# Cross-attention, two layers: new orders around o, and the low parts made on VectorE

## The chip, the cores and the metric

The kernel runs on 1 core of one Trainium2 chip. The metric is the device time of one execution in microseconds (us). The kernel before takes 1041.25 us, the median of 3 runs (1039.71 to 1041.26).

## The reference

x is (32, 224, 512), the context is (32, 750, 256), all in float32. Two layers follow each other; each computes, for every batch,

```
q = emb @ Wq + bq;  k = latent @ Wk + bk;  v = latent @ Wv + bv
w = softmax(q @ k.T / sqrt(512), axis=1)      # over the 224 rows of q, not over the context
x = w @ v + emb
out = (x - mean(x)) * rsqrt(var(x) + 1e-6) * gamma + beta
```

The second layer takes the first one's output as emb and the same context. Each has its own weights.

## The kernel before, in words

**Folding.** Wq and Wk are folded once into A, so that "q" is x times A with 256 columns, and scores are that q times the raw context. The values are folded too: first o = w @ context (256 columns), then o @ Wv, called pv. The bias of v is added with the row sum r of the probabilities.

**High and low parts.** Most products are split to keep float32 accuracy. A tensor t has a high part t_hi in the format fp32r, and t_lo = t - t_hi. A product is hi*hi + hi*lo + lo*hi. The high part is a conversion and the low part a subtraction that must see the high one finished. For o, only the first three of six chunks of 125 context rows are split: p_hi, p_lo (125x672, one buffer each) and raw_hi, raw_lo (125x384 for each half l of the columns, two slots by batch). The other three chunks are multiplied as they are.

**Units and turns.** A unit is one batch in one layer. A turn handles one unit of layer 0, called a, and one of layer 1, called b, which belongs to an earlier batch (in code a(+0) and b(+0), with a(-1), b(-1) for the turn before). There are 32 units of each layer. Some turns are written out, the middle ones are a loop of two turns. The first units and the last two have shapes of their own (opening, front_o_product, last_o_product).

**Order.** Each engine has a hand-written list, `turn(i, j)`, and runs it strictly in order. Semaphores tie the lists together. The steps that matter:

- TensorE (`turn` of the tensor block): score_product of a in three pairs of chunks, o_product of the earlier b (second half), two transposes of b's x, the pv and q products, then o_product(a, 0), spread_d(b), score_product(b, 0), (b, 1), o_product(a, 1), score_product(b, 2), q_product(a(+1), 0), pv_product(a, 0), spread_d, pv_product(a, 1), q_product(a(+1), 1), o_product(b, 0).
- VectorE takes the maxima of the scores (score_max, L1443), makes xT_lo (L1395), cT_lo, qT_lo (q_lo, L1426), oT_lo, the reciprocals (invert_sum, L1463), p_hi (probs_hi, L1479), raw_hi (L1491), the dots with a weight row (L1416), adds pv (add_pv, L1542), takes the moments (half_moments, L1559), and turns blocks of x and the context (turn_x, turn_ctx).
- ScalarE makes the high parts of transposed data, the exponentials (exps, L1023), scales the probabilities by the reciprocal (normalise, L1045), and standardises (L1080).
- GpSimd makes p_lo (L1864) and raw_lo (L1872), sums the probabilities (L1881 to L1896), takes the power -1/2 (L1941), and applies gamma and beta (L1958, L1967). SyncE issues the DMAs.

The waits of an o product are what the change touches most. o_product writes oq_bank[l], which has held the q of the next unit, so it first waits until VectorE has read that (q_lo):

```
if u.at(1).real:
    pe.wait_ge(qT_lo_done, u.n(1, 2, l - 1))
...
if u.layer == 0 or u.first:
    pe.wait_ge(raw_lo_done, u.batch(LC, l + 1))
if l == 0:
    pe.wait_ge(p_hi_done, u.n(add=-1))
```

Then it waits for the normalised second half of the probabilities ahead of L745, and for p_lo ahead of L749. q_product of b waits at L691 for xT_lo of b, its first half ahead of the first two products of the low part and its second half ahead of the other two. A GpSimd or VectorE step that needs the result of a step before it on the same engine waits for its semaphore as well.

Of the kernel before, what the change touches and what calls it, by code (L numbers as in the profile page):

```python
# [5 lines left out]
ALU = mybir.AluOpType  # L6
ACT = mybir.ActivationFunctionType
F32 = mybir.dt.float32
# [80 lines left out]
def build_xattn(nc, x, ctx, weights, out):  # L89
    B, T, E = x.shape  # L90
    _, M, L = ctx.shape
    P = 128
# [13 lines left out]
    with ExitStack() as stack:  # L106
# [821 lines left out]
        def _(act):  # L928
# [54 lines left out]
            def xT_hi_part(u, g):  # L983
                if not u.real:
                    return
                if u.layer:
                    act.wait_ge(xT_ready, u.batch(2, g + 1))
                    src = t_bank[0][:, 0:2 * T].rearrange("p (e t) -> p e t", e=2)
                else:
                    act.wait_ge(x_turned, u.batch(2, g + 1))  # L990
                    src = first_x(g) if u.first else turned_x(u, g)
                if u.past(-2) and g == 0:

                    act.wait_ge(q_ready, u.n(-2, 2))
                act.activation(xT_hi[:, u.par, 2 * g:2 * g + 2, :], src, ACT.Identity).then_inc(xT_hi_done, 1)  # L995
# [115 lines left out]
            def turn(i, j):  # L1111
                a, b = units(i, j)
                ctxT_hi(a(-1), 2)
                d_out(a(-1))
                standardise(a(-2), 0)
                standardise(a(-2), 1)
                ctxT_hi(a(-1), 3)
                o_hi(b(-2), 1)
                xT_hi_part(b(-1), 0)
                seed(b(-2), 1)  # L1120
                exps(a(-1), 0)
                xT_hi_part(b(-1), 1)
                xT_hi_part(a(+0), 0)
                exps(a(-1), 1)
                q_hi(b(-1), 0)
                normalise(a(-1), 0)
                normalise(a(-1), 1)
                q_hi(b(-1), 1)
                xT_hi_part(a(+0), 1)
                o_hi(a(-1), 0)  # L1130
                d_out(b(-1))
                seed(a(-1), 0)
                seed(a(-1), 1)
                exps(b(-1), 0)
                o_hi(a(-1), 1)
                standardise(b(-2), 0)
                standardise(b(-2), 1)
                ctxT_hi(a(+0), 0)
                q_hi(a(+0), 0)
                normalise(b(-1), 0)  # L1140
                exps(b(-1), 1)
                normalise(b(-1), 1)
                q_hi(a(+0), 1)
                ctxT_hi(a(+0), 1)
                seed(b(-1), 0)
                o_hi(b(-1), 0)
# [76 lines left out]
            seed(b29, 1)  # L1223
            exps(a31, 0)
            xT_hi_part(v, 1)
            exps(a31, 1)
            q_hi(v, 0)
            normalise(a31, 0)
            normalise(a31, 1)
            q_hi(v, 1)  # L1230
            o_hi(a31, 0)
# [45 lines left out]
        def _(dve):  # L1277
# [194 lines left out]
            def probs_hi(u):  # L1472

                if not u.real:
                    return
                dve.wait_ge(probs_done, u.n(m=2, add=-1))

                dve.wait_ge(o_ready, u.n(-1, 2))
                dve.tensor_copy(p_hi[0:MP, :, :], probs[0:MP, u.par4, 0:HALF, :]).then_inc(p_hi_done, 1)  # L1479

            def raw_hi_part(u, l):
# [8 lines left out]
                    dve.wait_ge(raw_loaded[u.slot][l], u.turns(16))  # L1490
                dve.tensor_copy(raw_hi[0:MP, u.slot, :, cols], raw[0:MP, u.slot, 0:HALF, cols]).then_inc(raw_hi_done, 1)  # L1491

            def take_r(u):

                if not u.real or not seeded(u):
                    return
                dve.wait_ge(oT_hi_done, u.n(m=2, add=R_HALF - 1))
                dve.wait_ge(y_done, u.n(-2, 2))
                dve.tensor_copy(r_col[0:TP, u.par, :], r_psum).then_inc(r_taken, 1)
# [114 lines left out]
            def turn(i, j):  # L1614
# [12 lines left out]
                score_max(b(-1), 4)  # L1627
                score_max(b(-1), 5)
                ctxT_lo(a(+0), 0)
                probs_hi(b(-1))  # L1630
                add_pv(a(-1), 0)
                q_lo(a(+0), 0)
                turn_ctx(a(+0), 1)
                invert_sum(b(-1), 1)
                half_moments(a(-1), 0)
                add_pv(a(-1), 1)
                half_moments(a(-1), 1)
# [20 lines left out]
                take_r(b(-1))  # L1658
                invert_sum(a(+0), 0)
                raw_hi_part(a(+0), 0)  # L1660
                score_max(a(+0), 5)
                xT_lo_part(b(+0), 1)
                dot(b(+0), 0)
                add_pv(b(-1), 0)
                q_lo(b(+0), 0)
                invert_sum(a(+0), 1)
                raw_hi_part(a(+0), 1)
                dot(b(+0), 1)
                probs_hi(a(+0))
                half_moments(b(-1), 0)  # L1670
                xT_lo_part(a(+1), 0)
                turn_x(a(+1), 1)
# [40 lines left out]
            turn_x(a1, 0)  # L1713
            o_lo(a0, 0)
            raw_hi_part(a0, 0)
            raw_hi_part(a0, 1)
            sum_beta(2)
            o_lo(a0, 1)
            sum_beta(3)
# [30 lines left out]
            score_max(a1, 5)  # L1750
            invert_sum(a1, 0)
            raw_hi_part(a1, 0)
            raw_hi_part(a1, 1)
            turn_x(a2, 0)
            fold_c(1, 1)
            xT_lo_part(b0, 1)
# [4 lines left out]
            dot(b0, 1)  # L1761
            q_lo(b0, 1)
            probs_hi(a1)
            xT_lo_part(a2, 0)
            turn_x(a2, 1)
            o_lo(a1, 0)
# [67 lines left out]
        def _(pool):  # L1834
# [10 lines left out]
            def first_sum_probs():  # L1845
                halves = [(probs[0:MP, 0, 0, :], 1), (psum3[0:MP, 0, :], 2), (psum3[0:MP, 0, :], 3), (psum3[0:MP, 0, :], 4),
                          (psum3[0:MP, 0, :], 5)]
                for k, (of, c) in enumerate(halves):
# [6 lines left out]
                        pool.tensor_tensor(psum_all[0:MP, :], of, probs[0:MP, 0, c, :], ALU.add).then_inc(psum_done, 1)  # L1855
                    else:
                        pool.tensor_tensor(psum3[0:MP, 0, :], of, probs[0:MP, 0, c, :], ALU.add).then_inc(first_psum_done, 1)

            def probs_lo(u):

                if not u.real or u.first and u.layer == 0:
                    return
                pool.wait_ge(p_hi_done, u.n(add=-1))
                pool.tensor_tensor(p_lo[0:MP, :, :], probs[0:MP, u.par4, 0:HALF, :], p_hi[0:MP, :, :].bitcast(F32),  # L1864
                                   ALU.subtract).then_inc(p_lo_done, 1)

            def raw_lo_part(u, l):
                if not u.real:
                    return
                cols = slice(l * P, (l + 1) * P)  # L1870
                pool.wait_ge(raw_hi_done, u.batch(LC, l + 1))
                pool.tensor_tensor(raw_lo[0:MP, u.slot, :, cols], raw[0:MP, u.slot, 0:HALF, cols],  # L1872
                                   raw_hi[0:MP, u.slot, :, cols].bitcast(F32), ALU.subtract).then_inc(raw_lo_done, 1)

            def sum_thirds(u):

# [92 lines left out]
            def turn(i, j):  # L1969
                a, b = units(i, j)  # L1970
                scale(b(-2), 1)
                probs_lo(b(-1))
                sum_thirds(b(-1))
                sum_two(b(-1))
                inverse_deviation(a(-1))
                sum_probs(b(-1))
                add_beta(b(-2), 0)
                add_beta(b(-2), 1)
                scale(a(-1), 0)
                add_beta(a(-1), 0)  # L1980
                scale(a(-1), 1)
                add_beta(a(-1), 1)
                raw_lo_part(a(+0), 0)
                raw_lo_part(a(+0), 1)
                probs_lo(a(+0))
                sum_thirds(a(+0))
                sum_two(a(+0))
                inverse_deviation(b(-1))
                sum_probs(a(+0))
                scale(b(-1), 0)  # L1990
# [49 lines left out]
```

## Time and profile before

| | before |
|---|---|
| median of 3 runs | 1041.25 us |
| the profiled execution, its own time | 1041.46 us |
| its span, first to last instruction | 1039.6 us |
| TensorE busy (matmuls) | 990.3 us, 95% |
| weight loads busy | 925.6 us, 89% |
| VectorE busy | 865.9 us, 83% |
| ScalarE busy | 727.0 us, 70% |
| GpSimd busy | 738.2 us, 71% |
| of which p_lo and raw_lo | 99.4 us in 61, 91.0 us in 64 |
| granted TensorE clock, mean | 0.996 |

Busy time says how full an engine is, not who waits for whom. The span is some 2 us shorter than the execution's own time. In the rows further down, PE is TensorE, DVE is VectorE, ACT is ScalarE and POOL is GpSimd. Matmuls are pipelined, so the start of one is more telling than its end.

### The profile page before, as it was taken

How to read it: one execution, taken by the hardware profiler on the slowest of the kernel's cores; microseconds unless marked ns; L12 is line 12 of the kernel's file. 1: busy time of each engine (PE TensorE's matmuls, PEld its weight loads, DVE VectorE, ACT ScalarE, POOL GpSimd, SP SyncE). 2: the span in 40 equal slices, each digit the busy share in tenths (PEclk: the TensorE clock that was granted, in tenths of full speed). 3: DMA queues.
4: the chain of work that ended last, by engine and by line, in shares of the span. 5: the costliest groups of instructions: out<-in, count | busy, mean ns of one | idle time of the engine just before them, and what ended most of it. 6: DMA issues, size and time to landing. Idle time of an engine off the chain costs nothing.

```text
span 1039.6 us, 25199 instructions
## 1 busy us (share of the span) xinstructions
PE 990.3 (95%) x7306; PEld 925.6 (89%) x7306; DVE 865.9 (83%) x2667; ACT 727.0 (70%) x2008; POOL 738.2 (71%) x646
## 2 busy tenths in 40 slices
PE   7989999999999999999999999999999999999997
PEld 6879899899899899899899899889889989989986
DVE  4879888889888888888888888888888888888867
ACT  2647777777776777776777776776777777677764
POOL 0336777778877777877777877778877778877784
PEclk9999999999999999999999999999999999999999
DMA  7744443454433455343455343445443345444211
GB/s 216 160 74 94 93 95 76 99 114 91 100 92 73 95 111 109 80 95 73 93 110 112 78 97 83 85 105 112 85 95 87 79 102 112 88 98 96 41 32 54
DMA packets 373961, 98.35 MB, mean 95 GB/s; under 512 B 308488, under 2 KB 357786, under 8 KB 373914
## 3 DMA queue, kind: packets, MB, share of 16 engines
q1 hardware_dynamic: 371370, 96.98, 42.5%
q10 hardware_dynamic: 2544, 0.80, 0.4%
q8 instruction: 23, 0.38, 0.1%
q14 instruction: 24, 0.20, 0.1%
HBM read 83.06 MB, written 14.68 MB: 94 GB/s over the span
## 4 chain that ended last, share of the span: by engine, by line
PE 52%; DVE 23%; ACT 12%; issue 6%; ACTq 0%; DVEq 0%
PE oq_bank L745 14%; PE score_bank L714 6%; ACT probs L1045 6%; PE score_bank L719 5%; PE score_bank L715 5%; DVE dot_junk L1416 4%; ACT probs L1023 4%; PE oq_bank L749 4%; PE oq_bank L740 4%; DVE p_hi L1479 4%; DVE y L1542 4%; PE oq_bank L741 3%; DVE xT_lo L1395 2%; DVE qT_lo L1426 2%; DVE raw_hi L1491 2%
## 5 line engine op out<-in xcount | busy, mean ns | idle before, releaser
L1023 ACT ACTIVATE probs<-probs,neg_max 125x224 f32<-125x224 f32 x378 | 177.8, 472 | 99.9 <-DVE neg_max L1443 99.7
L714 PE MATMUL score_bank<-qT_hi,cT_hi 128*125 128x224 f32 x768 | 198.0, 284 | 2.4 <-ACT qT_hi L1015 0.6
L715 PE MATMUL score_bank<-qT_hi,cT_lo 128*125 128x224 f32 x768 | 188.4, 272 | 0.0
L1045 ACT ACTIVATE probs<-probs,rsum 125x224 f32<-125x224 f32 x378 | 150.7, 471 | 24.0 <-DVE rsum L1463 23.9
L745 PE MATMUL oq_bank<-probs,raw 125*128 125x224 f32 x732 | 163.4, 360 | 3.4 <-ACT probs L1045 0.2
L1443 DVE CUSTOM_DVE_ANT_0 probs<-score_bank,d_row 125x224 f32<-125x224 f32 x384 | 139.9, 384 | 19.2 <-PE score_bank L719 14.8
L714 PEld LDWEIGHTS score_bank<-qT_hi,cT_hi 128*125 128x125 f32 x768 | 144.7, 188 | 7.0 <-issue 5.6
L719 PE MATMUL score_bank<-qT_lo,cT_hi 128*125 128x224 f32 x768 | 146.9, 272 | 0.0
L1958 POOL TENSOR_TENSOR y_out<-z,gamma_row 112x512 f32<-112x512 f32 x60 | 77.0, 1305 | 98.4 <-ACT z L1080 98.4
L1864 POOL TENSOR_TENSOR p_lo<-probs,p_hi 125x672 fp32r<-125x672 f32 x61 | 99.4, 1630 | 64.4 <-DVE p_hi L1479 64.4
L715 PEld LDWEIGHTS score_bank<-qT_hi,cT_lo 128*125 128x125 f32 x768 | 144.8, 189 | 0.0
L745 PEld LDWEIGHTS oq_bank<-probs,raw 125*128 125x128 f32 x732 | 130.0, 191 | 9.0 <-ACT probs L1045 8.8
L1881 POOL TENSOR_TENSOR psum<-probs 125x672 f32<-125x672 f32 x61 | 99.1, 1625 | 36.7 <-ACT probs L1045 36.7
L686 PE MATMUL oq_bank<-xT_hi,A_hi 128*128 128x224 f32 x512 | 120.7, 274 | 0.3 <-ACT xT_hi L995 0.2
L687 PE MATMUL oq_bank<-xT_hi,A_lo 128*128 128x224 f32 x512 | 120.9, 274 | 0.0
L740 PE MATMUL oq_bank<-p_hi,raw_hi 125*128 125x224 f32 x366 | 90.4, 280 | 28.6 <-DVE p_hi L1479 28.6
L719 PEld LDWEIGHTS score_bank<-qT_lo,cT_hi 128*125 128x125 f32 x768 | 114.6, 189 | 0.3 <-DVE qT_lo L1426 0.2
L995 ACT ACTIVATE xT_hi<-t_bank 128x448 fp32r<-128x448 f32 x128 | 65.5, 535 | 67.3 <-DVE t_bank L1360 61.9
L1872 POOL TENSOR_TENSOR raw_lo<-raw,raw_hi 125x384 fp32r<-125x384 f32 x64 | 91.0, 1423 | 24.6 <-DVE raw_hi L1491 24.6
L777 PE MATMUL pv_bank<-Wv_hi,oT_hi 128*112 128x512 f32 x256 | 105.3, 411 | 0.2 <-ACT oT_hi L1056 0.2
L686 PEld LDWEIGHTS oq_bank<-xT_hi,A_hi 128*128 128x128 f32 x512 | 97.8, 191 | 6.1 <-DVE w_col L1331 0.4
L687 PEld LDWEIGHTS oq_bank<-xT_hi,A_lo 128*128 128x128 f32 x512 | 97.9, 191 | 4.0
(164 smaller groups left out, 2796.5 us busy)
## 6 DMA issues: line engine op xcount, KB each, us to landing
raw<-in_ctx_dram SPq DMA_DIRECT2D x64, 375.0 KB
cb<-in_ctx_dram SPq DMA_DIRECT2D x248, 92.0 KB
x<-in_x_dram SPq DMA_DIRECT2D x32, 448.0 KB, 3.9
xb<-in_x_dram SPq DMA_DIRECT2D x124, 112.0 KB, 2.7
out_dram<-y_out SPq DMA_DIRECT2D x31, 448.0 KB, 6.2
cb<-in_ctx_dram SPq DMA_DIRECT2D x124, 3.5 KB
y<-in_L_xattn_Wq_dram SPq DMA_DIRECT2D x2, 512.0 KB, 5.3
probs<-in_L_xattn_Wq_dram SPq DMA_DIRECT2D x2, 512.0 KB, 12.1
```

What stands on the lines that cost most here:

```text
L686: nc.tensor.matmul(o, A_hi[:, u.layer, e, l * P:(l + 1) * P], xT_hi[:, u.par, e, :], start=(e == 0), stop=False)
L687: nc.tensor.matmul(o, A_lo[:, u.layer, e, l * P:(l + 1) * P], xT_hi[:, u.par, e, :], start=False, stop=False)
L714: nc.tensor.matmul(o, cT_hi[:, u.slot, l, cols], qT_hi[:, l, :], start=(l == 0), stop=False)
L715: nc.tensor.matmul(o, cT_lo[:, u.slot, l, cols], qT_hi[:, l, :], start=False, stop=False)
L719: ins = nc.tensor.matmul(o, cT_hi[:, u.slot, l, cols], qT_lo[:, l, :], start=False, stop=(l == LC - 1))
L740: nc.tensor.matmul(o, raw_hi[0:MP, u.slot, c, cols], p_hi[0:MP, c, :], start=(c == 0), stop=False)
L745: nc.tensor.matmul(o, raw[0:MP, u.slot, c, cols], probs[0:MP, u.par4, c, :], start=False, stop=False)
L777: nc.tensor.matmul(o, oT_hi[:, l, rows], Wv_hi[:, u.layer, l, :], start=(l == 0 and not seeded(u)), stop=False, skip_group_check=seeded(u))
L1023: ins = act.activation(probs[0:MP, u.par4, c, :], probs[0:MP, u.par4, c, :], ACT.Exp, bias=neg_max[0:MP, u.par4, c:c + 1], scale=-1.0, acc ...
L1045: ins = act.activation(probs[0:MP, u.par4, c, :], probs[0:MP, u.par4, c, :], ACT.Identity, scale=rsum[0:MP, u.par4, c:c + 1])
L1443: dve.tensor_tensor_reduce(probs[0:MP, u.par4, c, :], b[0:MP, (c % 2) * T:(c % 2 + 1) * T], d_row[0:MP, :], -SCALE, 3.4e38, ALU.add, ALU.m ...
L1864: pool.tensor_tensor(p_lo[0:MP, :, :], probs[0:MP, u.par4, 0:HALF, :], p_hi[0:MP, :, :].bitcast(F32), ALU.subtract).then_inc(p_lo_done, 1)
```

## The change

It does four things.

- probs_lo and raw_lo_part move from GpSimd to VectorE. On VectorE each stands directly behind its high part, and waits for it by the same semaphore. In the turn there are two probs_lo and two raw_lo_part; raw_lo_part also goes into the opening for the first two batches, and probs_lo for the first looped unit.
- ScalarE: normalise(a, 0) goes ahead of exps(a, 1); exps(b, 1) goes ahead of normalise(b, 0) and both ahead of q_hi(a(+1), 0).
- VectorE, for b: turn_ctx(.., 1) and invert_sum(b, 1) go ahead of probs_hi(b).
- VectorE, for a: probs_hi(a), with probs_lo(a), goes from behind dot(b, 1) to behind dot(b, 0); raw_hi_part(a, 1), raw_lo_part(a, 1) and invert_sum(a, 1) go ahead of q_lo(b, 0).

TensorE's and SyncE's lists and all data are the same.

```diff
--- before.py
+++ after.py
@@ -1121,9 +1121,9 @@
                 exps(a(-1), 0)
                 xT_hi_part(b(-1), 1)
                 xT_hi_part(a(+0), 0)
+                normalise(a(-1), 0)
                 exps(a(-1), 1)
                 q_hi(b(-1), 0)
-                normalise(a(-1), 0)
                 normalise(a(-1), 1)
                 q_hi(b(-1), 1)
                 xT_hi_part(a(+0), 1)
@@ -1136,9 +1136,9 @@
                 standardise(b(-2), 0)
                 standardise(b(-2), 1)
                 ctxT_hi(a(+0), 0)
+                exps(b(-1), 1)
+                normalise(b(-1), 0)
                 q_hi(a(+0), 0)
-                normalise(b(-1), 0)
-                exps(b(-1), 1)
                 normalise(b(-1), 1)
                 q_hi(a(+0), 1)
                 ctxT_hi(a(+0), 1)
@@ -1223,9 +1223,9 @@
             seed(b29, 1)
             exps(a31, 0)
             xT_hi_part(v, 1)
+            normalise(a31, 0)
             exps(a31, 1)
             q_hi(v, 0)
-            normalise(a31, 0)
             normalise(a31, 1)
             q_hi(v, 1)
             o_hi(a31, 0)
@@ -1490,6 +1490,22 @@
                     dve.wait_ge(raw_loaded[u.slot][l], u.turns(16))
                 dve.tensor_copy(raw_hi[0:MP, u.slot, :, cols], raw[0:MP, u.slot, 0:HALF, cols]).then_inc(raw_hi_done, 1)
 
+            def probs_lo(u):
+
+                if not u.real:
+                    return
+                dve.wait_ge(p_hi_done, u.n(add=-1))
+                dve.tensor_tensor(p_lo[0:MP, :, :], probs[0:MP, u.par4, 0:HALF, :], p_hi[0:MP, :, :].bitcast(F32),
+                                   ALU.subtract).then_inc(p_lo_done, 1)
+
+            def raw_lo_part(u, l):
+                if not u.real:
+                    return
+                cols = slice(l * P, (l + 1) * P)
+                dve.wait_ge(raw_hi_done, u.batch(LC, l + 1))
+                dve.tensor_tensor(raw_lo[0:MP, u.slot, :, cols], raw[0:MP, u.slot, 0:HALF, cols],
+                                   raw_hi[0:MP, u.slot, :, cols].bitcast(F32), ALU.subtract).then_inc(raw_lo_done, 1)
+
             def take_r(u):
 
                 if not u.real or not seeded(u):
@@ -1627,11 +1643,12 @@
                 score_max(b(-1), 4)
                 score_max(b(-1), 5)
                 ctxT_lo(a(+0), 0)
+                turn_ctx(a(+0), 1)
+                invert_sum(b(-1), 1)
                 probs_hi(b(-1))
+                probs_lo(b(-1))
                 add_pv(a(-1), 0)
                 q_lo(a(+0), 0)
-                turn_ctx(a(+0), 1)
-                invert_sum(b(-1), 1)
                 half_moments(a(-1), 0)
                 add_pv(a(-1), 1)
                 half_moments(a(-1), 1)
@@ -1658,15 +1675,18 @@
                 take_r(b(-1))
                 invert_sum(a(+0), 0)
                 raw_hi_part(a(+0), 0)
+                raw_lo_part(a(+0), 0)
                 score_max(a(+0), 5)
                 xT_lo_part(b(+0), 1)
                 dot(b(+0), 0)
+                probs_hi(a(+0))
+                probs_lo(a(+0))
                 add_pv(b(-1), 0)
+                raw_hi_part(a(+0), 1)
+                raw_lo_part(a(+0), 1)
+                invert_sum(a(+0), 1)
                 q_lo(b(+0), 0)
-                invert_sum(a(+0), 1)
-                raw_hi_part(a(+0), 1)
                 dot(b(+0), 1)
-                probs_hi(a(+0))
                 half_moments(b(-1), 0)
                 xT_lo_part(a(+1), 0)
                 turn_x(a(+1), 1)
@@ -1713,7 +1733,9 @@
             turn_x(a1, 0)
             o_lo(a0, 0)
             raw_hi_part(a0, 0)
+            raw_lo_part(a0, 0)
             raw_hi_part(a0, 1)
+            raw_lo_part(a0, 1)
             sum_beta(2)
             o_lo(a0, 1)
             sum_beta(3)
@@ -1750,7 +1772,9 @@
             score_max(a1, 5)
             invert_sum(a1, 0)
             raw_hi_part(a1, 0)
+            raw_lo_part(a1, 0)
             raw_hi_part(a1, 1)
+            raw_lo_part(a1, 1)
             turn_x(a2, 0)
             fold_c(1, 1)
             xT_lo_part(b0, 1)
@@ -1761,6 +1785,7 @@
             dot(b0, 1)
             q_lo(b0, 1)
             probs_hi(a1)
+            probs_lo(a1)
             xT_lo_part(a2, 0)
             turn_x(a2, 1)
             o_lo(a1, 0)
@@ -1856,22 +1881,6 @@
                     else:
                         pool.tensor_tensor(psum3[0:MP, 0, :], of, probs[0:MP, 0, c, :], ALU.add).then_inc(first_psum_done, 1)
 
-            def probs_lo(u):
-
-                if not u.real or u.first and u.layer == 0:
-                    return
-                pool.wait_ge(p_hi_done, u.n(add=-1))
-                pool.tensor_tensor(p_lo[0:MP, :, :], probs[0:MP, u.par4, 0:HALF, :], p_hi[0:MP, :, :].bitcast(F32),
-                                   ALU.subtract).then_inc(p_lo_done, 1)
-
-            def raw_lo_part(u, l):
-                if not u.real:
-                    return
-                cols = slice(l * P, (l + 1) * P)
-                pool.wait_ge(raw_hi_done, u.batch(LC, l + 1))
-                pool.tensor_tensor(raw_lo[0:MP, u.slot, :, cols], raw[0:MP, u.slot, 0:HALF, cols],
-                                   raw_hi[0:MP, u.slot, :, cols].bitcast(F32), ALU.subtract).then_inc(raw_lo_done, 1)
-
             def sum_thirds(u):
 
                 if not u.real or u.first and u.layer == 0:
@@ -1969,7 +1978,6 @@
             def turn(i, j):
                 a, b = units(i, j)
                 scale(b(-2), 1)
-                probs_lo(b(-1))
                 sum_thirds(b(-1))
                 sum_two(b(-1))
                 inverse_deviation(a(-1))
@@ -1980,9 +1988,6 @@
                 add_beta(a(-1), 0)
                 scale(a(-1), 1)
                 add_beta(a(-1), 1)
-                raw_lo_part(a(+0), 0)
-                raw_lo_part(a(+0), 1)
-                probs_lo(a(+0))
                 sum_thirds(a(+0))
                 sum_two(a(+0))
                 inverse_deviation(b(-1))
```

## Rows read from the trace of the kernel before

**Rows 1.** TensorE's waits: engine line waited for: us in total, times, longest

```profile
PE oq_bank L740 <- DVE p_hi L1479: 28.6, 31, 2.8
```

**Rows 2.** one turn: busy us (instructions) of each engine, clock, DMA share

```profile
500.20:531.20 31.00, 29.97 (x224) 28.06 (x225) 26.32 (x83) 22.45 (x62) 23.43 (x21) 1.00 0.43 94
```

**Rows 3.** timeline, TensorE: start us, us, line, operation [idle before <-releaser]

```profile
500.18 0.34 PE L740 MATMUL oq_bank<-p_hi,raw_hi 125*128 125x224 f32 x1 [0.81 <-DVE p_hi L1479]
...
514.70 0.27 PE L740 MATMUL oq_bank<-p_hi,raw_hi 125*128 125x224 f32 x1
...
527.02 0.61 PE L691 MATMUL oq_bank<-xT_lo,A_hi 128*128 128x224 f32 x4
...
529.75 0.61 PE L691 MATMUL oq_bank<-xT_lo,A_hi 128*128 128x224 f32 x4
531.22 0.34 PE L740 MATMUL oq_bank<-p_hi,raw_hi 125*128 125x224 f32 x1 [0.86 <-DVE p_hi L1479]
```

**Rows 4.** timeline, VectorE, from behind S to behind R

```profile
499.95 0.68 DVE L1559 BATCH_NORM_STATS2 bn<-y 112x6 f32<-112x512 f32 x1
...
505.88 0.38 DVE L1443 CUSTOM_DVE_ANT_0 probs<-score_bank,d_row 125x224 f32<-125x224 f32 x1
...
512.26 0.51 DVE L1479 CAST p_hi<-probs 125x672 fp32r<-125x672 f32 x1 [1.67 <-ACT probs L1045]
512.69 0.74 DVE L1542 SCALAR_TENSOR_TENSOR y<-bv_row,r_col,pv_bank 112x512 f32<-112x512 f32 x1
513.35 0.45 DVE L1426 SCALAR_TENSOR_TENSOR qT_lo<-oq_bank,c_col,qT_hi 128x224 fp32r<-128x224 f32 x1
```

**Rows 5.** timeline, ScalarE, same turn

```profile
506.31 0.48 ACT L1023 ACTIVATE probs<-probs,neg_max 125x224 f32<-125x224 f32 x1 [2.11 <-DVE neg_max L1443]
...
507.62 0.19 ACT L1023 ACTIVATION_READ_ACCUMULATOR probs<-probs,neg_max 125x1 f32 x1
...
509.51 0.47 ACT L980 ACTIVATE cT_hi<-t_bank 128x384 fp32r<-128x384 f32 x1
510.67 0.45 ACT L1015 ACTIVATE qT_hi<-oq_bank,c_col 128x224 fp32r<-128x224 f32 x1 [0.69 <-PE oq_bank L691]
511.02 1.22 ACT L1045 ACTIVATE probs<-probs,rsum 125x224 f32<-125x224 f32 x3
```

**Rows 6.** timeline, VectorE, from score_max(a, 4) to the end of the turn

```profile
524.71 0.39 DVE L1443 CUSTOM_DVE_ANT_0 probs<-score_bank,d_row 125x224 f32<-125x224 f32 x1
...
525.47 0.65 DVE L1491 CAST raw_hi<-raw 125x384 fp32r<-125x384 f32 x1
...
526.34 0.61 DVE L1395 TENSOR_TENSOR xT_lo<-t_bank,xT_hi 128x448 fp32r<-128x448 f32 x1
526.87 0.88 DVE L1416 CUSTOM_DVE_ANT_0 dot_junk<-z,w_row,c_col 112x512 f32<-112x512 f32 x1
...
528.35 0.44 DVE L1426 SCALAR_TENSOR_TENSOR qT_lo<-oq_bank,c_col,qT_hi 128x224 fp32r<-128x224 f32 x1
...
528.79 0.39 DVE L1491 CAST raw_hi<-raw 125x384 fp32r<-125x384 f32 x1
529.11 0.73 DVE L1416 CUSTOM_DVE_ANT_0 dot_junk<-z,w_row,c_col 112x512 f32<-112x512 f32 x1
...
529.77 1.30 DVE L1479 CAST p_hi<-probs 125x672 fp32r<-125x672 f32 x1
```

**Rows 7.** timeline, GpSimd, same turn

```profile
518.10 0.70 POOL L1941 TENSOR_TENSOR rstd<-ve,minus_half 112x2 f32<-112x2 f32 x1
...
524.52 1.31 POOL L1958 TENSOR_TENSOR x<-z,gamma_row 112x512 f32<-112x512 f32 x1
525.91 1.30 POOL L1967 TENSOR_TENSOR x<-x,beta_row 112x512 f32<-112x512 f32 x1
...
529.26 1.44 POOL L1872 TENSOR_TENSOR raw_lo<-raw,raw_hi 125x384 fp32r<-125x384 f32 x1 [0.63 <-DVE raw_hi L1491]
```

**Rows 8.** groups by shape, VectorE: busy us, mean ns, idle before

```profile
L1339 DVE TENSOR_TENSOR Wv_lo<-x,Wv_hi 128x1024 fp32r<-128x1024 f32 x1 | 1.2, 1197 | 0.0
```

## The prediction

> **Names.** A turn handles one layer-0 unit *a* and one layer-1 unit *b*. S is the start of TensorE's o_product(a, 0), R that of o_product(b, 0), S' the next S. "x(a', ..)" belongs to the following layer-0 unit and the layer-1 unit behind it.
>
> **What bounds the kernel now.** First the waits of TensorE: one line carries nearly everything, 28.6 us in 31 waits, for p_hi [rows 1]. Then one turn by busy time: of 31.0 us TensorE works 29.97, VectorE 26.32, GpSimd 23.43 [rows 2]. So TensorE is the bound with about 1 us of air per turn, and VectorE is second. The timeline of the same turn puts the air in one place: S at 500.18, R at 514.70, the last product ends at 529.75 + 0.61 = 530.36, and S' waits until 531.22 [rows 3]. The period is 31.04. What ends that wait is not ScalarE: the p_hi cast begins right behind a dot, so VectorE's queue is the cause. Its stretch from raw_hi at 525.47 to the end of the cast at 531.07 has no gap [rows 6]. Two of the durations there are stretched. The same cast takes 0.51 at 512.26 [rows 4] and 1.30 at 529.77 [rows 6], and the long one ends 0.37 behind the end of a GpSimd operation (529.26 + 1.44 = 530.70) [rows 7]. raw_hi takes 0.65 and 0.39 [rows 6]; the long one ends 0.29 behind GpSimd's 524.52 + 1.31 = 525.83. The dot from two SBUF operands at 526.87 takes 0.88, against 0.73 at 529.11 [rows 6], and ends 0.54 behind GpSimd's 527.21 [rows 7]. VectorE's cast and its two-SBUF operation wait until the running GpSimd operation is through.
>
> **The parts.** *Moved work.* raw_lo (125x384) and p_lo (125x672) come to VectorE, two of each per turn. Before has no such operation there; the nearest row is Wv_lo, a subtraction of two SBUF tensors, 1.20 us for 1024 elements [rows 8]. Estimate: 1024 elements at what the dot's 0.54 for 512 says are 1.08, so some 0.13 is fixed. p_lo is then 0.84 and raw_lo 0.54; each hides about 0.07 under its successor (529.11 + 0.73 against 529.77 [rows 6]), but must first see the end of the cast in front of it, some 0.12 lost (the overlap, and an estimated 0.04 of handover). That is 0.88 and 0.58, together 2.9 us a turn, on the engine with 4.7 us left. Ends of the price: 0.6 of this (the rate of the fast cast, 0.51 for 672) and 1.44 for the 384 elements, as on GpSimd [rows 7]; I take the Wv_lo row, the same kind of operation on the same engine. What goes from GpSimd is worth nothing by itself: it was off the path. It also takes away the raw_lo that p_hi(a) collided with, 0.8 us.
>
> *q_lo.* o_product(u, 0) writes the bank that holds the next unit's q, so it waits for that unit's q_lo(., 0). Before, q_lo(b, 0) ran at 528.35, well ahead of p_hi(a) [rows 6], and q_lo(a', 0) at 513.35, 1.35 ahead of R. After, both stand behind p_hi, p_lo and add_pv, the first also behind raw_hi, raw_lo and the reciprocal. So the wait for p_hi(a) becomes one for q_lo.
>
> *S to R.* If S is freed by q_lo(b, 0), VectorE still has dot(b, 1) (0.66 up to the next start [rows 6]) and everything from half_moments to score_max(b, 2), 505.88 + 0.39 - 499.95 = 6.32 [rows 4]. Started 0.2 before S this ends at S+6.8. ScalarE follows: exps(b, 0), o_hi, two standardise and cT_hi, 509.51 + 0.47 - 506.31 = 3.67 [rows 5], then exps(b, 1), now in front, 507.62 + 0.19 - 506.31 = 1.5, and normalise(b, 0) 1.22 [rows 5]: S+13.1 (overlaps of 0.08 taken off, a handover added). VectorE: p_hi 0.55 with its own wait, p_lo 0.76, add_pv 0.66 (513.35 - 512.69), q_lo 0.45 [rows 4]: S+15.55, TensorE at S+15.65. Now it is 14.52 [rows 3], which is TensorE's own work. New stall: 1.1. The idle 1.67 in front of p_hi(b) [rows 4] covers turn_ctx and the reciprocal, not this chain. normalise(b, 1) ends earlier than before, worth some tenths at L745; I leave it out. GpSimd is idle around p_hi(b) and p_lo(b): its scale has ended and sum_thirds waits for normalise(b, 1).
>
> *R to S'.* score_max(a', 4) hangs on TensorE: R+10.0 [rows 3, 6]. raw_hi starts at R+10.77 and ends at R+11.42 as now. GpSimd's block of add_beta and scale sits where it does: its reciprocal root at 518.10 [rows 7] waits for the same moments, which follow q_lo(a', 0) and therefore R. Its last add_beta (525.91 to 527.21) runs to R+12.51. raw_lo, ready at R+11.46, waits for that and ends 384/512 of 0.54 later, at R+12.92. Now xT_lo(b', 1) starts 0.22 behind raw_hi's end (526.34 against 526.12 [rows 6]); after, 0.22 behind raw_lo's, at R+13.14 instead of R+11.64, and ends at R+13.75. TensorE's L691, at R+12.32, needs it two products later, R+12.54: a second new stall, 1.3, which moves the end of q(b', 1) from R+15.66 to R+17.0. VectorE goes on without a gap: dot(b', 0) R+13.67, p_hi(a') 14.35, p_lo 14.90, add_pv 15.66, raw_hi 16.32, raw_lo 16.75, reciprocal 17.21, q_lo(b', 0) 17.29 to 17.74. normalise(a', 0), now ahead of exps(a', 1), is done by R+12.5 and hides. S' = R+17.85, against 16.52 now. GpSimd's idle stretch behind its block holds the later port users, so I charge no collision there.
>
> **The sum.** Period 15.65 + 17.85 = 33.5 against 31.04: +2.46. Of this +1.1 comes before R and +1.3 behind it. TensorE waits 31 times at L740 [rows 1], so there are 30 intervals: +74 us. The opening gets two raw_lo and one p_lo in front of the longest of these waits (2.8 [rows 1]), 2 x 0.58 + 0.88 = 2.0 at most, and two raw_lo earlier; I set that against the earlier normalise(b, 1), which I left out. The end of the run has none of the moved work. The profiled execution took 1041.46 (span 1039.6; the median of the runs is 1041.25), so 1041.5 + 74 = 1115.
>
> **Two rules of the Trainium skill.** The Trainium skill, "SBUF — State Buffer", section "Who interferes with whom": a VectorE instruction with two SBUF inputs contends with a GpSimd instruction that reads SBUF, and the one that comes second is blocked for the whole of the other. The dot above agrees (0.88 against 0.73). It speaks against this change, which puts such instructions where GpSimd runs back to back; without it the sum would be rival 1's. The Trainium skill, "GPSIMD Engine Reference", section "Elementwise" under its comparison with the Vector engine, has tensor_tensor on GpSimd 1.96 times slower; it speaks for the change, and by it GpSimd's 1.44 would be an estimated 0.73 on VectorE. No run here shows that pair yet.
>
> **Rivals.** *1. The subtraction doesn't wait for GpSimd* (the dot is another kind of operation). Then raw_lo ends at R+12.0, everything behind it is 0.92 earlier, S' = R+16.93, period 32.6, 30 x 1.54 = +46: 1088. For it: no row of before shows a two-SBUF subtraction against a busy GpSimd. Against it: cast and dot both wait, to within 0.02 of the same end. 15%.
> *2. Slack takes most of it up.* If VectorE keeps S near where it was (its queue is shorter than my chain by some tenths at several handovers), R stays at S+14.5 and only the net of the stretch behind score_max counts: removed are a dot 0.66, the stretched cast 0.8, the dot's 0.14; added are raw_lo twice and p_lo, 2.0: +0.4 a turn, 1054; down to 1041 with the L745 wait gone. For it: ScalarE idles 0.69 before q_hi(a') [rows 5] and TensorE has 0.86 at S. Against: S to R is a chain without a gap. 11%.
> *3. Faster.* The planned effect alone: p_hi is ready earlier, the 28.6 us at L740 go, nothing replaces them: 1041.5 - 28.6 = 1013. It decides if q_lo(b, 0) is done before R+15.66, which needs my VectorE chain to be 2.1 us too long. For it: 0.8 + 0.26 + 0.14 of stretched operations go if GpSimd is out of the way, and TensorE's floor is 29.97. Against: GpSimd's block hasn't moved. 7%, with small gains in it.
> *4. Worse*: the lag also brings the later port users, or the moments, against GpSimd, half a us or more a turn: 1130 to 1145. 8%.
> The forecast has 59%.
>
> **Numbers.** 1115. The range 1055 to 1135 leaves out rival 3, most of rival 2 and part of rival 4. No change means within 0.2% (2 us, what a measurement can tell). Faster 0.08, same 0.02 (the lower end of rival 2), slower 0.90.
>
> **What would show it.** Right: TensorE's L740 waits not for p_hi but for q_lo's line, twice a turn, about 1 us each; L691 waits some 1.3 for xT_lo; raw_lo(a, 0) takes near 1.5 us and ends 0.4 behind a GpSimd add_beta, its second sister 0.54; the period is near 33.5 and VectorE is busy near 28 of it. Wrong: raw_lo takes 0.54 both times (rival 1), S to R stays 14.5 (rival 2), or L740 waits for nothing (rival 3).

## The result: 1117.26 us, 7.4% slower

The changed kernel takes 1117.26 us (median of 4 runs, 1116.64 to 1118.54) against 1041.26 us (4 runs, 1039.71 to 1041.43) for the kernel before. The ratio is 1.0735, with a 95% interval of 1.0716 to 1.0754. The prediction was 1115.

One turn of it, as in [rows 2]: length, then the busy us of TensorE, its weight loads, VectorE, ScalarE and GpSimd.

```profile
502.92:536.47 33.55, 30.23 (x224) 28.17 (x225) 29.47 (x87) 22.11 (x63) 17.41 (x16) 1.00 0.40 87
```

A turn is 33.55 us long instead of 31.04. TensorE does the same 30 us of work in it and waits for the rest; VectorE is busy 29.5 instead of 26.3; GpSimd has 6 us less to do.

TensorE's waits (line, what it waited for, us in total, times, longest), which answer to [rows 1]:

```profile
PE oq_bank L740 <- DVE qT_lo L1426: 38.7, 52, 1.2
PE oq_bank L691 <- DVE xT_lo L1395: 32.0, 30, 2.2
PE score_bank L714 <- DVE cT_lo L1387: 14.9, 22, 0.7
PE oq_bank L740 <- issue: 6.7, 8, 0.8
...
PE oq_bank L740 <- DVE p_hi L1479: 3.5, 1, 3.5
```

The 28.6 us for p_hi have become 3.5, all of it in the opening. In their place stand waits for q_lo (L740, twice a turn), for xT_lo (L691), and one that the prediction did not have, for cT_lo at the first score product of a'. "issue" is a wait that the profile puts down to no engine; the eight here stand at S, where q_lo is waited for in the other turns. The timeline of TensorE, same turn, answers to [rows 3]:

```profile
502.92 0.34 PE L740 MATMUL oq_bank<-p_hi,raw_hi 125*128 125x224 f32 x1 [1.09 <-DVE qT_lo L1426]
...
518.08 0.37 PE L740 MATMUL oq_bank<-p_hi,raw_hi 125*128 125x224 f32 x1 [0.48 <-DVE qT_lo L1426]
...
521.16 0.34 PE L714 MATMUL score_bank<-qT_hi,cT_hi 128*125 128x224 f32 x1 [0.68 <-DVE cT_lo L1387]
...
532.19 0.48 PE L691 MATMUL oq_bank<-xT_lo,A_hi 128*128 128x224 f32 x2 [1.09 <-DVE xT_lo L1395]
...
536.47 0.34 PE L740 MATMUL oq_bank<-p_hi,raw_hi 125*128 125x224 f32 x1 [1.08 <-DVE qT_lo L1426]
```

S to R is 15.16 and R to S' 18.39; before they were 14.52 and 16.52.

VectorE from score_max(a', 4) to q_lo(b', 0), which answers to [rows 6], and GpSimd beside it, [rows 7]:

```profile
529.16 1.53 DVE L1491 CAST raw_hi<-raw 125x384 fp32r<-125x384 f32 x1
530.73 0.56 DVE L1506 TENSOR_TENSOR raw_lo<-raw,raw_hi 125x384 fp32r<-125x384 f32 x1
...
531.51 0.62 DVE L1395 TENSOR_TENSOR xT_lo<-t_bank,xT_hi 128x448 fp32r<-128x448 f32 x1
532.05 0.74 DVE L1416 CUSTOM_DVE_ANT_0 dot_junk<-z,w_row,c_col 112x512 f32<-112x512 f32 x1
...
532.72 0.51 DVE L1479 CAST p_hi<-probs 125x672 fp32r<-125x672 f32 x1
533.26 0.86 DVE L1498 TENSOR_TENSOR p_lo<-probs,p_hi 125x672 fp32r<-125x672 f32 x1
...
534.69 0.42 DVE L1491 CAST raw_hi<-raw 125x384 fp32r<-125x384 f32 x1
535.14 0.56 DVE L1506 TENSOR_TENSOR raw_lo<-raw,raw_hi 125x384 fp32r<-125x384 f32 x1
...
535.70 0.42 DVE L1426 SCALAR_TENSOR_TENSOR qT_lo<-oq_bank,c_col,qT_hi 128x224 fp32r<-128x224 f32 x1
```

```profile
527.74 1.30 POOL L1967 TENSOR_TENSOR x<-z,gamma_row 112x512 f32<-112x512 f32 x1
529.12 1.29 POOL L1976 TENSOR_TENSOR x<-x,beta_row 112x512 f32<-112x512 f32 x1
```

There is no gap from 529.16 to 536.12, 6.96 us. raw_hi takes 1.53 instead of its own 0.42 (534.69): GpSimd's add_beta ends at 529.12 + 1.29 = 530.41, and the cast ends 0.28 behind it, the 0.29 of [rows 6, 7] over again. The cast had come 0.04 us behind the start of that GpSimd operation.

Not every turn is like this one. In 22 of them, the looped ones, raw_hi takes the wait. In 7 others, the first and the last of the run, raw_lo takes it, and the turn is 33.05 us long instead of 33.55:

```profile
128.21 1.48 DVE L1506 TENSOR_TENSOR raw_lo<-raw,raw_hi 125x384 fp32r<-125x384 f32 x1
```

Over the whole run (busy us, mean ns):

```profile
L1498 DVE TENSOR_TENSOR p_lo<-probs,p_hi 125x672 fp32r<-125x672 f32 x61 | 52.7, 864 | 2.1
...
L1491 DVE CAST raw_hi<-raw 125x384 fp32r<-125x384 f32 x64 | 49.2, 768 | 0.0
...
L1506 DVE TENSOR_TENSOR raw_lo<-raw,raw_hi 125x384 fp32r<-125x384 f32 x64 | 42.1, 658 | 2.2
...
L1479 DVE CAST p_hi<-probs 125x672 fp32r<-125x672 f32 x61 | 31.7, 519 | 27.4 <-ACT probs L1045 27.4
```

p_lo takes 0.86 in every turn, raw_lo 0.56 when free. p_hi is stretched in no turn any more, only once in the opening (1.25); its mean was 900 ns.

### The profile page after: what moved, and what is told of

It reads as the page before. It is cut to its first block, busy times and chain, and to the rows that moved or that the text cites. A ratio compares the mean times of both kernels' runs of the same rounds, so it can differ in the third digit from the quotient of the medians.

```text
span 1115.0 us, 25188 instructions
## 1 busy us (share of the span) xinstructions
PE 1000.6 (90%) x7306; PEld 927.5 (83%) x7306; DVE 957.1 (86%) x2792; ACT 717.1 (64%) x2008; POOL 551.4 (49%) x521
## 4 chain that ended last, share of the span: by engine, by line
DVE 33%; PE 31%; ACT 15%; issue 14%; DVEq 0%; ACTq 0%
ACT probs L1023 8%; PE oq_bank L745 7%; DVE y L1558 6%; DVE raw_hi L1491 4%; PE score_bank L714 4%; DVE xT_lo L1395 4%; DVE bn L1575 3%; PE score_bank L719 3%; PE score_bank L715 3%; DVE dot_junk L1416 3%; ACT z L1080 2%; DVE probs L1443 2%; PE oq_bank L740 2%; ACT probs L1045 2%; DVE p_hi L1479 2%
## 5 line engine op out<-in xcount | busy, mean ns | idle before, releaser
L714 PE MATMUL score_bank<-qT_hi,cT_hi 128*125 128x224 f32 x768 | 198.5, 285 | 19.1 <-DVE cT_lo L1387 14.9
L1045 ACT ACTIVATE probs<-probs,rsum 125x224 f32<-125x224 f32 x378 | 153.8, 473 | 71.8 <-DVE rsum L1463 71.8
L714 PEld LDWEIGHTS score_bank<-qT_hi,cT_hi 128*125 128x125 f32 x768 | 144.7, 188 | 25.0 <-issue 23.7
L745 PE MATMUL oq_bank<-probs,raw 125*128 125x224 f32 x732 | 160.9, 356 | 0.0
L719 PE MATMUL score_bank<-qT_lo,cT_hi 128*125 128x224 f32 x768 | 147.0, 272 | 0.0
L740 PE MATMUL oq_bank<-p_hi,raw_hi 125*128 125x224 f32 x366 | 93.6, 289 | 48.9 <-DVE qT_lo L1426 38.7
L745 PEld LDWEIGHTS oq_bank<-probs,raw 125*128 125x128 f32 x732 | 130.0, 192 | 1.4 <-ACT probs L1045 1.3
L740 PEld LDWEIGHTS oq_bank<-p_hi,raw_hi 125*128 125x128 f32 x366 | 70.3, 192 | 59.3 <-DVE raw_lo L1506 27.3
L719 PEld LDWEIGHTS score_bank<-qT_lo,cT_hi 128*125 128x125 f32 x768 | 114.6, 189 | 0.3 <-DVE qT_lo L1426 0.2
L691 PE MATMUL oq_bank<-xT_lo,A_hi 128*128 128x224 f32 x512 | 85.9, 280 | 32.0 <-DVE xT_lo L1395 32.0
L1395 DVE TENSOR_TENSOR xT_lo<-t_bank,xT_hi 128x448 fp32r<-128x448 f32 x128 | 78.9, 617 | 34.4 <-ACT xT_hi L995 34.2
## 6 DMA issues: line engine op xcount, KB each, us to landing
probs<-in_L_xattn_Wq_dram SPq DMA_DIRECT2D x2, 512.0 KB, 12.9
```

Source lines behind the costliest of these rows:

```text
L714: nc.tensor.matmul(o, cT_hi[:, u.slot, l, cols], qT_hi[:, l, :], start=(l == 0), stop=False)
L719: ins = nc.tensor.matmul(o, cT_hi[:, u.slot, l, cols], qT_lo[:, l, :], start=False, stop=(l == LC - 1))
L740: nc.tensor.matmul(o, raw_hi[0:MP, u.slot, c, cols], p_hi[0:MP, c, :], start=(c == 0), stop=False)
L745: nc.tensor.matmul(o, raw[0:MP, u.slot, c, cols], probs[0:MP, u.par4, c, :], start=False, stop=False)
L1045: ins = act.activation(probs[0:MP, u.par4, c, :], probs[0:MP, u.par4, c, :], ACT.Identity, scale=rsum[0:MP, u.par4, c:c + 1])
L1395: dve.tensor_tensor(xT_lo[:, u.par, 2 * g:2 * g + 2, :], src, xT_hi[:, u.par, 2 * g:2 * g + 2, :].bitcast(F32), ALU.subtract).then_inc(xT_ ...
```

## The experiments

Ten kernels, each timed in rounds beside the kernel before on the same chip. Ratios are to that kernel, with their 95% intervals. Its medians beside them were 1040.7 to 1041.7 us, so times of different experiments can be compared to about 1 us.

**e1, the orders alone.** The lists of ScalarE and VectorE are the new ones; probs_lo and raw_lo_part stay on GpSimd. VectorE's list for a:

```diff
+                probs_hi(a(+0))
                 add_pv(b(-1), 0)
+                raw_hi_part(a(+0), 1)
+                invert_sum(a(+0), 1)
                 q_lo(b(+0), 0)
...
-                probs_hi(a(+0))
```

> The new orders of ScalarE and VectorE, with both low parts left on GpSimd. Theory (the loss is the load on VectorE, its collisions with GpSimd, and q_lo standing behind it): the orders alone are close to neutral. p_hi(a) casts about 0.7 us earlier, but the next o product then waits for q_lo(b, 0), which ends near where p_hi ended, and for p_lo, which GpSimd makes behind two raw_lo. R-S 14.5 to 14.8, period 30.8 to 31.4, 1035 to 1052 us. Rival (the orders themselves are the fault, the moved work is free): the whole loss is here, period near 33.5, about 1115 us.

Measured: 1045.26 us, ratio 1.0039 (1.0026 to 1.0053). The waits moved, as they should, and hardly changed in sum:

```profile
PE score_bank L714 <- DVE cT_lo L1387: 10.4, 22, 0.5
PE oq_bank L749 <- POOL p_lo L1864: 9.6, 29, 0.4
PE oq_bank L691 <- DVE xT_lo L1395: 7.2, 14, 1.0
...
PE oq_bank L740 <- DVE p_hi L1479: 2.8, 1, 2.8
```

The rival is gone: the orders are not the fault by themselves.

**e2, the move alone.** The changed kernel with the orders of before. VectorE's list for a, against the kernel before (p_lo(b) stands behind p_hi(b) in the same way):

```diff
                 raw_hi_part(a(+0), 0)
+                raw_lo_part(a(+0), 0)
...
                 raw_hi_part(a(+0), 1)
+                raw_lo_part(a(+0), 1)
                 dot(b(+0), 1)
                 probs_hi(a(+0))
+                probs_lo(a(+0))
```

> The low parts on VectorE directly behind their high parts, with the orders of the kernel before. Theory: most of the loss is here. raw_hi and raw_lo of the first half meet GpSimd's back-to-back block (+1.5 ahead of xT_lo(b, 1), so L691 waits about 1.2), the second pair and p_lo add 1.4, the cast of p_hi(a) gets 0.8 back: S'-R 17.6, R-S 14.6 to 14.9, period 32.3, about 1080 us; TensorE waits for p_hi at L740, not for q_lo. Rival (orders are the fault): 1041 to 1050 us.

Measured: 1147.80 us, ratio 1.1024 (1.1005 to 1.1042), 68 us more than expected. The move costs 106 us with the old orders and 72 (1117 against 1045) with the new. TensorE waited in four places:

```profile
PE oq_bank L691 <- DVE xT_lo L1395: 34.4, 30, 2.2
PE oq_bank L745 <- ACT probs L1045: 26.5, 30, 0.9
PE oq_bank L740 <- DVE p_hi L1479: 26.1, 31, 2.4
PE score_bank L719 <- DVE qT_lo L1426: 23.2, 29, 0.8
```

What I had not charged is p_lo(a): here it stands behind the normalised second half, at the moment when GpSimd starts its sum over the same probabilities. VectorE, then GpSimd:

```profile
510.07 1.47 DVE L1506 TENSOR_TENSOR raw_lo<-raw,raw_hi 125x384 fp32r<-125x384 f32 x1
...
516.33 2.16 DVE L1498 TENSOR_TENSOR p_lo<-probs,p_hi 125x672 fp32r<-125x672 f32 x1
```

```profile
509.83 1.29 POOL L1976 TENSOR_TENSOR x<-x,beta_row 112x512 f32<-112x512 f32 x1
516.04 1.73 POOL L1890 TENSOR_TENSOR psum<-probs 125x672 f32<-125x672 f32 x1 [4.92 <-ACT probs L1045]
```

p_lo takes 2.16 instead of 0.86 and ends 0.72 behind GpSimd's 517.77; raw_lo takes 1.47 and ends 0.42 behind GpSimd's 511.12. The two differ by 0.30 us for 288 elements, 1.04 ns each. Over the run p_lo is busy 91.7 us instead of 52.7, which is 39 of the 68 us; the rest was not taken apart. So the two-SBUF subtraction does wait, and rival 1 of the prediction falls.

**e3, q_lo(b, 0) earlier.** Changed kernel, one step moved.

```diff
                 add_pv(b(-1), 0)
+                q_lo(b(+0), 0)
                 raw_hi_part(a(+0), 1)
                 raw_lo_part(a(+0), 1)
                 invert_sum(a(+0), 1)
-                q_lo(b(+0), 0)
```

> The changed kernel with one step moved: q_lo(b, 0) directly behind add_pv, ahead of the second raw_hi, raw_lo and the reciprocal. Theory (the place of q_lo sets S'): the wait of L740 behind q(b, 1), 1.1 us a turn, goes; S' becomes TensorE's own or that of the late normalise, the period falls by 0.8 to 1.1 to about 32.6, 30 turns, 1083 to 1093 us. The wait of L691 stays. Rival (VectorE's total load sets the period, wherever q_lo stands): it stays within 5 us of 1117.

Measured: 1126.09 us, ratio 1.0820 (1.0802 to 1.0838): slower by 9 us, where the theory had some 30 less and the rival the same time: both missed. q_lo was one blocker of two. The reciprocal now stands last, the normalise it frees follows, and L745 waits where L740 did:

```profile
PE oq_bank L745 <- ACT probs L1045: 34.3, 30, 1.3
PE oq_bank L691 <- DVE xT_lo L1395: 30.4, 30, 2.2
...
PE oq_bank L740 <- DVE qT_lo L1426: 13.8, 30, 1.2
```

**e4, no block on GpSimd in front of raw_hi.** Changed kernel with GpSimd's add_beta of layer 0 cut short.

```diff
-                pool.tensor_tensor(o, o, beta_row[0:TP, u.layer, :], ALU.add).then_inc(ln_done, 1)
+                w = E if u.layer else 8
+                pool.tensor_tensor(o[:, 0:w], o[:, 0:w], beta_row[0:TP, u.layer, 0:w], ALU.add).then_inc(ln_done, 1)
```

> The changed kernel, in which GpSimd adds beta of layer 0 to 8 of 512 columns only (that part of the computation is left out), so that its block of back-to-back operations is over before VectorE comes to raw_hi(a, 0). VectorE's list and load are the same. Theory (collision on the way to SBUF): raw_hi(a, 0) falls from 1.53 to 0.42 us, the 1.1 us wait of L691 goes, period 32.4 to 32.6, 1083 to 1090 us. Rival (the cast is slow for another reason, or VectorE's load alone sets the period): raw_hi stays near 1.5, or the time stays within 5 us of 1117.

Measured: 1087.65 us, ratio 1.0447 (1.0429 to 1.0464), 29.6 us less than the changed kernel, or 0.99 in each of 30 turns. VectorE's list and its own work are untouched, and:

```profile
L1506 DVE TENSOR_TENSOR raw_lo<-raw,raw_hi 125x384 fp32r<-125x384 f32 x64 | 35.7, 558 | 2.2
...
L1491 DVE CAST raw_hi<-raw 125x384 fp32r<-125x384 f32 x64 | 26.0, 407 | 0.0
```

The casts fall from 768 to 407 ns, the subtractions from 658 to 558: 64 x 0.46 = 29.5 us. L691 waits 2.5 us in all instead of 32.0, and TensorE's other waits stay as they were (q_lo at L740 38.7, cT_lo at L714 14.9), so the shorter add_beta acted here only. This is the collision, measured by itself: no element less was subtracted.

**e7, q_lo and the reciprocal both earlier.** What e3 called for.

```diff
                 add_pv(b(-1), 0)
+                invert_sum(a(+0), 1)
+                q_lo(b(+0), 0)
                 raw_hi_part(a(+0), 1)
                 raw_lo_part(a(+0), 1)
-                invert_sum(a(+0), 1)
-                q_lo(b(+0), 0)
```

> The changed kernel with the reciprocal (a, 1) and q_lo(b, 0) both ahead of the second raw_hi and raw_lo. Theory (after e3: behind q_lo the next blocker is the reciprocal, whose normalise L745 waits for, so both must move): the 1.1 us wait at S goes, no wait of that size at L745, period 32.5 to 32.9, 1085 to 1098 us. Rival (VectorE's load sets the period): above 1110 us.

Measured: 1115.11 us, ratio 1.0702 (1.0686 to 1.0719), 2 us better than the changed kernel; the range is missed and the rival (above 1110) holds. The wait at S is gone, as expected, and paid back:

```profile
PE oq_bank L691 <- DVE xT_lo L1395: 30.5, 30, 2.2
PE oq_bank L740 <- DVE qT_lo L1426: 24.8, 30, 1.2
...
PE score_bank L719 <- DVE qT_lo L1426: 9.5, 29, 0.3
```

The 24.8 us at L740 are now at R: 0.81 a time (0.48 in the changed kernel), and L719 has 0.33 that it had not. The second raw_hi and raw_lo were only put behind S, in front of the same VectorE steps that lead to R. My theory of a place falls here. What holds is a loop: from score_max(a, 4) over S to R the chain through VectorE (and ScalarE, ahead of p_hi(b)) has no slack, so a step put elsewhere inside it moves the waits and does not shorten the period. It can lengthen it, as e3's 9 us show.

**e8, raw_lo back on GpSimd,** p_lo kept on VectorE.

The first two cuts are of VectorE's list, the last is of GpSimd's.

```diff
                 raw_hi_part(a(+0), 0)
-                raw_lo_part(a(+0), 0)
...
                 raw_hi_part(a(+0), 1)
-                raw_lo_part(a(+0), 1)
...
                 add_beta(a(-1), 1)
+                raw_lo_part(a(+0), 0)
+                raw_lo_part(a(+0), 1)
```

> The changed kernel with raw_lo returned to GpSimd and p_lo kept on VectorE. Theory: VectorE loses 2 x 0.5 us and the 1.5 us that raw_hi and raw_lo spend against GpSimd's block ahead of xT_lo; p_hi and the dot meet GpSimd's raw_lo instead. Period near 32, 1062 to 1078 us. With the orders alone at 1045 and the whole change at 1117, the larger part of the difference is then raw_lo's. Rival (p_lo on VectorE is the costly one): above 1095 us.

Measured: 1096.82 us, ratio 1.0531 (1.0513 to 1.0549), outside the theory's range and just inside the rival's (above 1095). Returning raw_lo gives 20 us, 0.68 a turn. VectorE's busy time explains it: it loses raw_lo's 42.1 us and 9.7 of raw_hi, but the dots with z grow by 20.7 and p_hi by 13.6, because they now meet raw_lo on GpSimd (one dot runs 1.29); with the rest it falls from 957.1 to 938.0, 19 us. raw_hi(a, 0) still takes some 1.5 in 12 of the turns:

```profile
519.95 1.53 DVE L1491 CAST raw_hi<-raw 125x384 fp32r<-125x384 f32 x1
...
525.76 1.29 DVE L1416 CUSTOM_DVE_ANT_0 dot_junk<-z,w_row,c_col 112x512 f32<-112x512 f32 x1
```

I had counted that wait as raw_lo's; where it falls depends on when in the turn the cast comes.

**e9, short subtractions.** Changed kernel, p_lo and raw_lo cut short on VectorE.

```diff
-                cols = slice(l * P, (l + 1) * P)
+                cols = slice(l * P, l * P + 8)
...
+                dve.tensor_tensor(p_lo[0:MP, :, 0:8], probs[0:MP, u.par4, 0:HALF, 0:8], p_hi[0:MP, :, 0:8].bitcast(F32),
```

> The changed kernel, in which VectorE makes p_lo of 24 of its 672 columns and raw_lo of 24 of its 384 columns only (the rest stays zero, so most of the low parts is left out; GpSimd clears both buffers once at the start). Every step, wait and order is as in the changed kernel. After e3 and e7 the theory reads: from score_max(a, 4) over S to R VectorE's queue has no slack, so each us of its work or waiting there is a us of the period, and which wait shows it does not matter. Taken away are 2 x 0.68 + 2 x 0.38 = 2.1 us a turn; raw_hi(a, 0) still waits for GpSimd. Period 31.3 to 31.8, 1048 to 1064 us. Rival (the waits for the cast's own semaphore and the port set the period, not the subtractions' length): above 1090 us.

Measured: 1055.33 us, ratio 1.0144 (1.0129 to 1.0160), 62 us less than the changed kernel, 2.06 a turn, for 2.1 us of VectorE's time taken out a turn. The orders are in place and so is the collision (the casts still take 721 ns in the mean). TensorE no longer waits for q_lo at L740 (0.7 us in all); what is left are xT_lo at L691 (19.1) and cT_lo (15.0). So the time that VectorE spends on the subtractions is paid for one for one.

The elements are not the whole loss, though: e4 got 30 us back with all of them in place, and 62 and 30 are more than the 76 lost; one reason is that the change had also shortened the casts of p_hi (busy 54.9 before, 31.7 now). What the runs share is VectorE's busy time, from their pages, here less the changed kernel's 957.1 and 1116.8 us:

| | VectorE busy | time of the profiled execution |
|---|---|---|
| e9, short subtractions | -62.3 us | -62.4 us |
| e4, no block on GpSimd | -30.2 | -28.7 |
| e8, raw_lo back | -19.1 | -20.7 |
| e7, both earlier | -3.9 | -1.1 |
| e3, q_lo earlier | -3.5 | +7.9 |
| e2, the orders of before | +34.6 | +32.2 |

Only e3 departs from it by more than 3 us. Back to the kernel before the rule is looser, 91.2 us busy for 75.4 of time: VectorE's idle time ahead of p_hi, 47.7 us in all before and 27.4 now, took up some of the added work.

**e5, the other way.** The kernel before, low parts on GpSimd, two swaps.

```diff
                 raw_hi_part(a(+0), 1)
+                probs_hi(a(+0))
                 dot(b(+0), 1)
-                probs_hi(a(+0))
...
                 raw_lo_part(a(+0), 0)
+                probs_lo(a(+0))
                 raw_lo_part(a(+0), 1)
-                probs_lo(a(+0))
```

> The kernel before with two swaps only: VectorE casts p_hi(a) ahead of dot(b, 1), and GpSimd makes p_lo(a) ahead of raw_lo(a, 1). Low parts stay on GpSimd. Theory (what bounds the kernel before is VectorE's queue in front of p_hi(a), with its cast held up by raw_lo(a, 1) on GpSimd): the cast starts at its normalise, takes 0.51, and the 0.86 us in front of L740 goes nearly whole: period 30.2 to 30.5, 1016 to 1026 us. Rival (p_lo on GpSimd or the next dot becomes the new wait): L749 waits for p_lo, 1035 to 1045 us.

Measured: 1015.90 us (5 runs, 1015.80 to 1016.75), ratio 0.9755 (0.9742 to 0.9769). It beats both kernels. Of 30.2 us TensorE works 29.98, and L740 has its wait of the opening left:

```profile
500.00:530.20 30.20, 29.98 (x226) 27.98 (x225) 25.66 (x82) 22.32 (x64) 23.36 (x20) 1.00 0.45 96
```

```profile
PE oq_bank L740 <- DVE p_hi L1479: 2.8, 1, 2.8
```

**e6, e5 with normalise(a, 0) ahead of exps(a, 1).**

```diff
+                normalise(a(-1), 0)
                 exps(a(-1), 1)
                 q_hi(b(-1), 0)
-                normalise(a(-1), 0)
```

> As the run before it, with ScalarE's normalise(a, 0) also ahead of exps(a, 1), as in the changed kernel. Theory: p_hi(a) is then held by nothing but VectorE's queue, some 0.3 us earlier, which TensorE at its own pace can hardly use: within 4 us of e5. If the order of ScalarE matters by itself (normalise(a, 1) comes late and L745 waits), it is slower than e5 by more than that.

Measured: 1024.88 us, ratio 0.9846 (0.9830 to 0.9862), 9 us slower than e5, against less than 4 expected. VectorE's q_lo(b, 0), ahead of the cast in its queue, waits for q_hi, which now stands behind three more activations; in e5 and before that group had 2.0 us in 4 waits. TensorE's S then comes 0.76 us behind the start of its last group at L691 instead of 0.45, 0.3 a turn.

```profile
DVE qT_lo L1426 <- ACT qT_hi L1015: 20.9, 33, 0.9
```

**e10, only VectorE's swap of e5.**

```diff
                 raw_hi_part(a(+0), 1)
+                probs_hi(a(+0))
                 dot(b(+0), 1)
-                probs_hi(a(+0))
```

> Of the two swaps of e5 only VectorE's: p_hi(a) ahead of dot(b, 1); GpSimd keeps raw_lo(a, 1) ahead of p_lo(a). Theory (the cast waits for the running GpSimd operation): raw_lo(a, 1) starts at once behind its raw_hi, so the cast is held until about 0.2 us before S and part of the gain goes: period 30.4 to 30.8, 1022 to 1034 us. Rival (only the place of the dot matters): within 3 us of e5, 1016.

Measured: 1036.09 us, ratio 0.9959 (0.9945 to 0.9972), a little above the range given. The cast in e10, GpSimd beside it, TensorE behind it, and then the cast in e5:

```profile
526.41 1.21 DVE L1479 CAST p_hi<-probs 125x672 fp32r<-125x672 f32 x1 [0.24 <-ACT probs L1045]
```

```profile
526.25 1.01 POOL L1872 TENSOR_TENSOR raw_lo<-raw,raw_hi 125x384 fp32r<-125x384 f32 x1 [0.62 <-DVE raw_hi L1491]
```

```profile
527.76 0.34 PE L740 MATMUL oq_bank<-p_hi,raw_hi 125*128 125x224 f32 x1 [0.40 <-DVE p_hi L1479]
```

```profile
517.61 0.51 DVE L1479 CAST p_hi<-probs 125x672 fp32r<-125x672 f32 x1 [0.25 <-ACT probs L1045]
```

raw_lo(a, 1) has started 0.16 earlier and holds the cast for 0.7 us; 20 of the 26 us are in GpSimd's swap. In both kernels the cast waits about 0.25 for its normalise before that. The expectation left out p_lo: in e10 it ends at 529.76, and L749 starts at 529.81, 2.05 behind S, against 1.71 in the kernel before.

## Why the prediction was right

The time came within 2.3 us. The parts came within 0.6 us each, not all for the reasons given, and part of the closeness is luck: two errors cancelled.

- **Moved work**: p_lo 0.84, measured 0.86; raw_lo 0.54, measured 0.56. The Wv_lo row was the right neighbour.
- **S to R**: 15.65, measured 15.16. p_hi(b) was cast at S+12.7, not S+13.1. VectorE entered S 0.2 further on than I put it, and ScalarE's steps from exps(b, 0) to normalise(b, 0) took 6.05, not 6.3, since each starts before the one ahead has ended.
- **R to S'**: 17.85, measured 18.39. The cT_lo wait of 0.68 was missing. ctxT_lo(a', 1) stands behind add_pv and two moments, all pushed back with q_lo(a', 0), and I checked only q_lo there. It moved raw_hi(a', 0) from R+10.77 to R+11.08. The other 0.24 is at S' itself: TensorE starts 0.35 behind the end of q_lo(b', 0), where I had 0.11. In the turns at both ends of the run that gap is 0.10 and the wait ahead of L714 is 0.39; why the loop's are longer is not shown.
- **The collision**: total right, place wrong in 22 turns and right in 7. I had the wait on raw_lo, with raw_hi stretched by 0.26 as before. In the looped turns raw_hi met the next add_beta and took the wait itself, and raw_lo ran free. It took two shifts: raw_hi came 0.31 later, and add_beta started at R+11.04, 0.17 earlier than the R+11.21 of before. With add_beta where I had put it, raw_hi at R+11.08 would still have come ahead of it. raw_lo ended at R+13.2 instead of R+12.9, and L691 waited 1.09 instead of 1.3. e4 prices it at 1.0 a turn.
- **q_lo as what frees S**: right as an observation, wrong as a cause. Moving it away gained nothing: 9 us more in e3, 2 less in e7. The two errors of half a us cancelled in the period, 33.5 against 33.55.
- **Nothing for the work taken off GpSimd**: right in the sum; GpSimd gained 6 us a turn and the turn grew by 2.5. But the 0.17 comes from there. The prediction says that GpSimd's reciprocal root at 518.10 waits for the moments. They were ready at 517.54; it stood behind GpSimd's own sum, which the lighter queue has out of the way:

```profile
517.48 0.67 POOL L1889 TENSOR_TENSOR psum<-psum 125x224 f32<-125x224 f32 x1
```

```profile
521.33 0.70 POOL L1950 TENSOR_TENSOR rstd<-ve,minus_half 112x2 f32<-112x2 f32 x1 [1.87 <-DVE ve L1589]
```

The first row is of the kernel before, the second of the changed one, where the root does wait for the moments.

- **The opening**: put at nothing, two effects set against each other. S of the first turn came at 67.50 instead of 65.26, 2.2 us later; the 30 intervals behind it gave 73.2 of the 74.
- **The new orders**: +4 us (e1), which the prediction did not price apart.
- **Rivals**: 1 falls by e2 (2.16 and 1.47 us next to GpSimd). 2 needed S to R to stay at 14.5; it is 15.16. 3 named a gain that was there: e5 has it, by the swap of two neighbours instead of a move of work. 4 had the right mechanism for another kernel: e2 is that case.

What stays open: 29 of e2's 68 us, and why the loop's turns are half a us longer than the others. Whether p_lo could move to VectorE under e5's orders was not tried.

## What to carry to other kernels

Where TensorE waits for the second busiest engine, look whether that engine's queue is the loop. Here the time that a change added to that queue, anywhere between the wait and the next one, priced it to 3 us in five runs of six, and the step that the waiting line names did not. The exception, e3, moved a step that another engine needed. Before moving work to relieve a conflict, try swapping the two operations that meet; here two swaps were worth 26 us and the move cost 76. And follow each step pushed back to its own reader: the one left out is the next wait.

## What the runs showed of the hardware

In these runs a VectorE cast or two-SBUF operation that meets a running GpSimd one ends a fixed time behind it: 0.29 and 0.28 for the cast of 384 elements (before, after), 0.42 for a two-SBUF subtraction of 384 (after at 128.21, e2) and 0.72 for one of 672 (e2). That a subtraction with two SBUF inputs is held by a GpSimd operation that reads SBUF is what the Trainium skill states in "SBUF — State Buffer", section "Who interferes with whom", and e2 agrees (2.16 against 0.86 us). New to me was how much a little time decides. A cast that came 0.04 us behind the start of a GpSimd operation waited for all of it (1.53); one that came 0.23 ahead of such a start (the changed kernel at 127.74) took 0.43, and the subtraction behind it carried the wait. GpSimd is lengthened too: its p_lo takes 2.06 instead of 1.63 us where a dot has just started (e5, e10), and raw_lo, 1.42 in the mean before, takes 1.00 where nothing is in its way (e8).
